# Blocked causal attention: GpSimd zeroes the masked half of the diagonal blocks after the exponential, in place of TensorE's mask products of the second pass

## The reference, cut to what matters

```python
x = x + 0.5 * L0_ffn(layernorm(x))
x = x + L0_attn(layernorm(x), w_qkv, w_out)   # the stage of this change
x = x + 0.5 * L0_ffn(layernorm(x))            # ... and eight more stages
# inside L0_attn, for one batch of 256 tokens and one head:
# scores = q @ k.T * HD ** -0.5; a query sees the keys up to its own place
# att = softmax(scores) @ v ; all heads' att @ w_out
```

## Time and profile before

| what | value |
|---|---|
| median of 3 runs | 3186.45 us (3180.18 to 3190.23) |
| span of the profiled execution | 3040.8 us |
| PE busy | 2525.0 us (83%) |
| DVE busy | 2108.5 us (69%) |
| ACT busy | 1803.5 us (59%) |
| POOL busy | 1186.1 us (39%) |
| pass B's mask products, PE busy (L2004) | 47.2 us, 512 products of 178 ns |

### The profile page before, as it was taken

How to read it: one execution, slowest core, us unless ns; L and a number is a source line. 1 busy time by engine, 2 the same in 40 slices (tenths; PEclk the granted TensorE clock), 3 DMA queues, 4 the chain that set the end, 5 groups by cost and what they waited for, 6 DMA issues and landing times.

```text
span 3040.8 us, 67855 instructions
## 1 busy us (share of the span) xinstructions
PE 2525.0 (83%) x25429; PEld 1994.5 (66%) x25429; DVE 2108.5 (69%) x7749; ACT 1803.5 (59%) x3508; POOL 1186.1 (39%) x1634
## 2 busy tenths in 40 slices
PE   7889989759599777569489999999999986693886
PEld 4466665447377555346378999999999874462655
DVE  6667765863378833854488888888888887445877
ACT  5344445434255333446279999999999974462553
POOL 4200002576532657566662222222222235656412
PEclk9799998879799788779799999999999997796997
DMA  9900000014210133325100000000000001351001
GB/s 237 283 19 3 3 3 1 13 54 141 68 48 3 40 106 114 97 83 177 55 27 13 2 13 10 4 14 1 13 14 1 2 1 34 102 168 41 27 3 29
DMA packets 148390, 157.20 MB, mean 52 GB/s; under 512 B 15585, under 2 KB 123746, under 8 KB 148066
## 3 DMA queue, kind: packets, MB, share of 16 engines
q1 hardware_dynamic: 119618, 78.14, 9.6%
q0 software_dynamic: 28448, 74.71, 7.7%
HBM read 77.79 MB, written 75.01 MB: 50 GB/s over the span
## 4 chain that ended last, share of the span: by engine, by line
PE 39%; DVE 11%; POOL 5%; issue 3%; DMA 1%; ACT 1%; POOLq 0%; DVEq 0%; ACTq 0%
PE banks L3246 7%; PE banks L3261 7%; PE banks L3191 3%; POOL bins L2984 3%; PE banks L3227 2%; PE banks L3200 2%; PE banks L3208 2%; PE banks L3226 2%; PE banks L3184 2%; PE banks L3022 1%; PE banks L3023 1%; PE banks L3033 1%; PE banks L3024 1%; PE banks L3035 1%; POOL results L1441 1%
## 5 line engine op out<-in xcount | busy, mean ns | idle before, releaser
L3343 POOL TENSOR_SCALAR shared_floats<-shared_floats 128x2 f32<-128x2 f32 x256 | 57.3, 224 | 658.1 <-DVE shared_floats L3334 657.9
L3261 PE MATMUL banks<-layer,shared_floats 128*128 128x128 f32 x2048 | 291.2, 275 | 0.0
L3261 PEld LDWEIGHTS banks<-layer,shared_floats 128*128 128x128 f32 x2048 | 258.8, 192 | 0.0
L3246 PE MATMUL banks<-shared_floats,layer 128*128 128x256 f32 x1024 | 245.8, 383 | 0.0
L3582 ACT ACTIVATE shared_floats<-banks,layer 128x256 f32<-128x256 f32 x512 | 210.2, 470 | 52.1 <-PE banks L3246 52.1
L3246 PEld LDWEIGHTS banks<-shared_floats,layer 128*128 128x128 f32 x1024 | 187.6, 193 | 20.8
L3345 POOL TENSOR_TENSOR shared_floats<-shared_floats,neg_half 128x2 f32<-128x2 f32 x256 | 183.2, 715 | 21.3
L1361 POOL DMA_INDIRECT results<-shared_floats,e_token_rows x160 | 155.0, 969 | 88.3 <-issue 48.2
L3355 DVE TENSOR_SCALAR shared_floats<-banks,shared_floats 128x128 f32<-128x128 f32 x512 | 185.8, 404 | 4.0 <-POOL shared_floats L3345 4.0
L244 PE MATMUL banks<-ident,xn 128*128 128x128 f32 x320 | 62.3, 327 | 141.5 <-issue 81.6
L2133 DVE TENSOR_REDUCE shared_floats<-banks 128x2 f32<-128x512 f32 (+3 forms) x256 | 110.7, 484 | 94.2 <-PE banks L1997 93.0
(11 more groups left out here) (398 smaller groups left out, 7968.0 us busy)
## 6 DMA issues: line engine op xcount, KB each, us to landing
bins<-zero SPq DMA_DIRECT2D x1, 18176.0 KB, 69.5
bins<-layer SPq DMA_DIRECT2D x16, 650.0 KB, 12.2
shared_floats<-bins SPq DMA_DIRECT2D x32, 325.0 KB, 3.4
expert_weights<-in_dram_experts SPq DMA_DIRECT2D x32, 312.0 KB, 3.0
results<-results SPq DMA_DIRECT2D x32, 256.0 KB, 3.2
layer<-in_dram_layers SPq DMA_DIRECT2D x8, 902.0 KB, 4.5
results<-zero SPq DMA_DIRECT2D x1, 4096.0 KB, 16.1
bins<-xn,f_bin_row POOLq DMA_INDIRECT x256, 2.3
```

Source lines behind the costliest of these rows:

```text
L3246: m = T.matmul(k.bank[5 + half][:, part], w["w1"][:, tile(n)], h1[:, :], start=True, stop=True)
L3261: m = T.matmul(to, hidden[:, n * S + t * P:n * S + (t + 1) * P], w["w2"][:, tile(n)], start=False, stop=(n == NF - 1), skip_group_check=True)
```

## The change

The mask products of pass B (L2004) are gone; the product that subtracts the maxima now ends the group (`stop=True`), and it raises `at_scored_b`. The exponential is therefore taken of unmasked scores. The eight exponential buffers become slices of one tensor, `at_exps`, so that two neighbouring ones can be reached in one instruction. GpSimd gets `mask_exps`: for each pair of exponentials it waits for `at_exps`, then issues for each block of the round four `affine_select` instructions, one for each 32 partitions, on 2 x 32 columns (the diagonal block in both buffers), which put zero where the key is ahead of the query. The last one raises a semaphore (`constants_made`, from 2 on). `weigh` waits for that semaphore and no longer for `at_exps`. The norm's roots on GpSimd are moved into the same list of jobs, at the job "stats", behind a wait for all masking issued so far, and each is followed by a wait for its own end.

```diff
--- before.py
+++ after.py
@@ -1945,6 +1945,15 @@
 
     return [k.sb(f"at_{name}{c % 2}", [P, width]) for name, width in
             (("q", CH), ("k", CH), ("q_heads", 4 * CH), ("k_heads", 4 * CH), ("v_heads", 4 * CH))]
+
+
+def att_exps(k, unit):
+    return k.sb("at_exps", [P, 8 * CH])[:, unit % 8 * CH:(unit % 8 + 1) * CH]
+
+
+def exps_masked(k):
+
+    return k.sem("constants_made"), 2
 
 
 def softmax_tensor(k, s, a):
@@ -1998,11 +2007,8 @@
                                    mask(k, "ahead_a", r)[:, 0:ahead], start=False, stop=True, skip_group_check=True)
             if i < len(blocks_b):
                 for r in rows_b:
-                    T.matmul(k.bank[6 + r % 2][:, at_b:at_b + wide_b], mask(k, "minus", r),
-                             shifts[rows32(r), begin_b:end_b], start=False, stop=False, skip_group_check=True)
-                for r in rows_b:
-                    m_b = T.matmul(k.bank[6 + r % 2][:, at_b:at_b + BK], mask(k, "same", r), mask(k, "ahead_b", r),
-                                   start=False, stop=True, skip_group_check=True)
+                    m_b = T.matmul(k.bank[6 + r % 2][:, at_b:at_b + wide_b], mask(k, "minus", r),
+                                   shifts[rows32(r), begin_b:end_b], start=False, stop=True, skip_group_check=True)
                 at_b += wide_b
         if first is not None:
             m_a.then_inc(k.sem("at_scored_a"), 1)
@@ -2020,10 +2026,11 @@
             if n:
                 T.wait_ge(k.sem("at_att"), a.g0 + n)
         if begin == 0:
-            T.wait_ge(k.sem("at_exps"), a.u0 + n * a.units + 4 * rd + 4)
+            masked, made = exps_masked(k)
+            T.wait_ge(masked, made + n * a.slots + 2 * rd + 2)
         for b, first, last in blocks[begin:end]:
             blk, width = n % 2 * BLOCKS + b, last - first
-            exps = [k.sb(f"at_exps{(n * a.units + 4 * rd + r) % 8}", [P, CH])[:, at:at + width] for r in range(4)]
+            exps = [att_exps(k, n * a.units + 4 * rd + r)[:, at:at + width] for r in range(4)]
             begins, ends = first == 0, b == BLOCKS - 1
             for r in range(4):
                 T.matmul(to[rows32(r), first:last], v_heads[:, blk * P + 32 * r:blk * P + 32 * r + 32], exps[r],
@@ -2235,7 +2242,7 @@
         if 2 * g >= 8:
             A.wait_ge(k.sem("at_weighed"), a.r0 + (2 * g - 8) // 4 + 1)
         for r in rows:
-            A.activation(k.sb(f"at_exps{(n * a.units + 4 * rd + r) % 8}", [P, CH])[:, 0:width],
+            A.activation(att_exps(k, n * a.units + 4 * rd + r)[:, 0:width],
                          k.bank[6 + r % 2][:, 0:width], ACT.Exp, scale=SCALE).then_inc(k.sem("at_exps"), 1)
 
     def copy_shifts(n):
@@ -2268,10 +2275,42 @@
 
 def softmax_gpsimd(k, s, a):
 
-    for c in range(s.early, NC):
-        ln_rstd(k, s, c)
-    for j in range(NC):
-        early_root(k, s, j)
+    G, (masked, made) = k.nc.gpsimd, exps_masked(k)
+
+    def mask_exps(n, p):
+
+        n, rd, rows, g = a.pair(n, p, True)
+        unit = (n * a.units + 4 * rd + rows[0]) % 8
+        both = k.sb("at_exps", [P, 8 * CH])[:, unit * CH:(unit + 2) * CH].rearrange("p (r n) -> p r n", n=CH)
+        G.wait_ge(k.sem("at_exps"), a.u0 + 2 * g + 2)
+        at = 0
+        for _, first, last in a.rounds_b[rd]:
+            for j in range(4):
+                block = both[rows32(j), :, at:at + BK]
+                m = G.affine_select(out=block, in_=block, compare_op=ALU.is_ge, fill=0.0, base=0,
+                                    pattern=[[0, 2], [1, BK]], channel_multiplier=-1)
+            at += last - first
+        m.then_inc(masked, 1)
+
+    if not s.early:
+        ln_rstd(k, s, 0)
+        G.wait_ge(k.sem("ln_rstd"), s.ln(0) + 1)
+    for n in range(B + a.lag):
+        c, odd = n // 2, n % 2
+        for job, i, behind in a.order:
+            if job == "score" and a.pair(n, i, True) is not None:
+                mask_exps(n, i)
+            if job == "stats":
+                done = sum(a.pair(m, p, True) is not None for m in range(n + 1) for p in range(a.slots) if (m, p) < (n, 2))
+                if done:
+                    G.wait_ge(masked, made + done)
+                if max(s.early, 1) <= c + 1 < NC and not odd:
+                    ln_rstd(k, s, c + 1)
+                    G.wait_ge(k.sem("ln_rstd"), s.ln(c + 1) + 1)
+                if n >= 2 * NC - 2:
+                    early_root(k, s, n - (2 * NC - 2))
+                    if s.next and n - (2 * NC - 2) < s.next.early:
+                        G.wait_ge(k.sem("ln_rstd"), s.next.ln(n - (2 * NC - 2)) + 1)
 
 
 CAUSAL_A = [[(b, 0, 256) for b in (6, 7)], [(b, 0, 192) for b in (4, 5)],
```

## The result

The changed kernel took 3252.11 us (median of 4 runs, 3247.22 to 3252.18) against 3183.31 us of the kernel before (median of 4, 3173.89 to 3190.23): ratio 1.0228, 95% interval 1.0206 to 1.0249. It is 69 us or 2.3% slower. The forecast was 3198 us, with a range up to 3233.

A forecast was written before the change was run, and what follows sets the result against it. PE was taken to set the pace, with DVE close behind. Contention 8 x 1.7 = 13.6, plus 1.5 at the stage's end, less 3.5 gained, gave +11.6 us: 3186.45 to 3198 us, range 3180 to 3233.

The forecast's parts named there:

- the selects run one by one: Rival for the selects on POOL: start-to-start spacing 0.19 to 0.24 us, total 3218 to 3233 us, chance 0.23.
- The bound of the pace: Selects on POOL: start-to-start spacing x lies between 0.04 and 0.24 us, from memsets and one 128 x 128 select.
- x = 0.13: Selects on POOL: forecast start-to-start spacing in us, near the middle of the bounds, as four neighbours may overlap.
- quadrants running side by side: Rival for the selects on POOL: full overlap of the four gives x = 0.08 and 3187 us, chance 0.33.
- 0.16 + 11x + 0.28: Masks ahead of `weigh`: us from the exponentials until a burst of 12 selects is ready, x being their start-to-start spacing.
- taken at nothing: Wait of `weigh` in round 0: no cost, with only 8 selects against a slack of about two scores.
- the late `weigh` of round 1 lies in the same stretch of the loop and hides in it: Wait of `weigh` in round 1: late by 0.1 and 0.2 us, adding nothing beyond the 1.7 us charged for contention.
- The contention: DVE's `parts` beside a burst of selects: 1.1 us overlap per batch, 1.7 us per two batches after cover, 13.6 in all.
- behind DVE's addition of 0.69 us as well: Term of the one-by-one rival: round 1's burst delayed by DVE's addition in one batch of two, 8 x 0.69 us.
- The end of the stage: Where the batches run out: fewer jobs between exponential and `weigh` cost 1.5 us, between 0 and 4.
- The gain: Removal of 512 mask products from PE: 3.5 us saved, with ends 0 and 4.8, from 0.03 us per pair.
- The roots at "stats": Norm's roots on POOL, with the next masks behind them: no cost unless x is over 0.19.

The follow-up runs named there:

- e6_whole: Changed kernel with one always-true select per block over all 128 partitions instead of four over 32, pass B unmasked: 3035.03 us, ratio 0.9981 to the kernel before.
- e9_by_quadrant: Changed kernel with the same 1024 selects issued quadrant by quadrant instead of block by block: 3210.43 us against 3177.49 of the kernel before, ratio 1.0095.
- e10_scratch_roots: Kernel before plus 1024 selects on a scratch tile, awaited only by GpSimd, roots issued ahead of round 2's second burst: 3181.87 us against 3177.49, ratio 1.0013.
- e5_after_again: The changed kernel, unedited, run again: 3114.32 us against 3041.59 of the kernel before, ratio 1.0246.
- e1_before_again: The kernel before, unedited, traced again on a quicker chip: span 3036.5 us, 3037.96 us in the run beside it.
- e2_no_masking: Changed kernel without the GpSimd selects, pass B unmasked, weigh waiting for the exponentials: 3030.72 us against 3039.37 of the kernel before, ratio 0.9967.

## Why the prediction was wrong

The direction and the mechanism (selects one by one, `weigh` waits for them) were in it, as the rival "the selects run one by one", with a chance of 0.23 and 3218 to 3233. The forecast itself, +11.6 us, was built on another mechanism: it was contention between the selects and DVE's `parts` (13.6 us of it), with the wait of `weigh` put at nothing. What the runs show is the reverse, a wait of 6.4 us in two batches and little contention. The measured 69 us lie above the whole range, the rival included. By steps:

1. **The bound of the pace.** "These bound the pace x ... 0.04 to 0.24 us" failed. The upper end was the spacing behind one select of 128 x 128, with twice our elements in each partition and four times the partitions, and so it looked safe. Measured: 0.28. From start to start it is 0.19, as estimated for one alone, as long as the next one works on the same partitions; with a change of quadrant the next starts 0.05 us after the last has ended. The row of the bound had a successor that works on all partitions as it does, and could not show this.

2. **Where I took the middle.** x = 0.13 rested on quadrants running side by side in part. No overlap of quadrants shows in any trace. The rule of the Trainium skill that spoke for it ("GPSIMD Engine Reference", section Instruction dispatch: a core begins the next instruction as soon as its own share of the last is done) is not borne out in its effect here: e6_whole and e9_by_quadrant show that neighbours on different partitions follow each other later than those on the same.

3. **The wait, and that it would hide.** The formula 0.16 + 11x + 0.28 was right: with 0.28 it gives 3.5 us, and 3.44 to 3.45 were measured. Round 1 is late by 1.7 us, round 2 by 0.9 and more, and even round 0, "taken at nothing", by 0.2: its 8 selects are ready 2.41 us behind the exponentials, against a slack of 2.13 to 2.25 us before. What failed is "the late `weigh` of round 1 lies in the same stretch of the loop and hides in it". It doesn't hide: PE's idle time in two batches goes from 3.4 to 9.1 us, 6.4 more by the new wait and 0.7 less by the old ones. With 0.8 us of products gone that makes 4.9, and 43.93 - 39.07 is 4.9. The rival left the wait of round 1 out of its sum too: with 0.28 for x its terms give some +53 us (an estimate: 8 x 3.9 of contention, 16 x 1.0 for round 2, 8 x 0.69, 4, less 3.5), still too low, and with contention as the largest of them.

4. **The contention.** 1.1 us for each batch at x = 0.13 (up to 2.2 at 0.24) was the largest term, and it failed. The wait for DVE's maxima was to grow from 3.3 us to about 5 and shrank to 2.4. DVE's `parts` in the changed kernel starts at 318.21 and its last four products are over at 320.59:

```profile
318.21 0.17 DVE L2158 CAST at_high<-shared_floats 128x32 bf16<-128x32 f32 x1
...
320.05 0.54 DVE L2161 TENSOR_TENSOR at_parts<-shared_floats,same_head 128x32 bf16<-128x32 f32 x4
```

It takes 2.38 us instead of 2.19, and 2.48 in every second batch, while POOL issued select after select. The longest of its products takes 0.27 us in the changed kernel against 0.19 before. A small operation that meets a select is held up by some tens of ns, at most 0.08 us. The earlier trace rows showed the hold-up behind a POOL operation with two inputs over all partitions, and I carried it over to selects with one input over a quarter of them; which of the two differences matters was not tried. All contention of DVE with the selects together is some 4 us or less (e10_scratch_roots).

   The other way round there is a hold-up that the forecast left out and the rival named ("behind DVE's addition of 0.69 us as well"). DVE's addition over 128 x 512, both inputs in SBUF, makes the select that starts inside it take up to 0.64 us instead of 0.23, 12 times in the stage. Here the first select of a burst starts 0.23 us behind the addition's start, and the burst of 12 takes 3.65 us instead of 3.32:

```profile
310.83 0.69 DVE L2129 TENSOR_TENSOR shared_floats<-shared_floats 128x512 f32<-128x512 f32 x1
...
311.06 3.65 POOL L2290 TENSOR_SCALAR_AFFINE_SELECT shared_floats<-shared_floats 32x64 f32<-32x64 f32 x12 [1.16 <-ACT shared_floats L2245]
```

   Where such a burst is one that `weigh` waits for, in round 2 of every second batch, `weigh` starts 3.85 us behind the exponentials and not 3.45.

5. **The clock, which was not in the sum.** In the changed kernel PE is granted the lower level now and then from about 177 us on; the kernel before has 1.00 in all windows of its steady part. Two batches with such stretches take 45.59 and 47.15 us against 43.93 without: 1.7 and 3.2 us. From `parts` of the second batch to `parts` of the last, 14 batches, it is 321.3 us in e5_after_again (175.6 to 497.0, mean clock 0.94) against 269.7 in e1_before_again (176.4 to 446.2, mean clock 0.99), 51.6 more. Seven times 4.9 is 34, which leaves some 18 us for the clock; at a mean clock of 0.94 the work of PE loses 6% of 321 us, 19 us, which is about as much. The four runs of e5_after_again point the same way: the one of this trace, with a mean clock of 0.907 over the program, took 3105.83 us, the three with 0.896 and 0.897 took 3112.58 to 3119.09.

   What PE did before the falls was to stand in the waits for GpSimd that the kernel before doesn't have: in the trace of the changed kernel each of the eight falls between 200 and 440 us comes 1.4 to 2.8 us after the start of such a wait of 1.35 to 1.73 us. But the same waits stand between 315.67 and 359.60 us, where the clock stays at 1.00, so they are not enough by themselves. With the shorter bursts of e9_by_quadrant, PE's longest idle time there is 1.35 us, and the clock kept 1.00. That the waits are the cause is the likeliest reading, not a shown one, since no run kept the waits and filled them with work for PE.

6. **The end of the stage.** 1.5 us was the estimate, 4 the upper end. From `parts` of the last batch to the last product of `weigh` it takes 35.3 us in e5_after_again (mean clock 0.65) against 21.6 in e1_before_again (0.92), 13.8 more. But the trace of before takes 31.8 us for it at a clock of 0.54, and the changed kernel's first trace 36.4 at 0.56. So at like clocks it is some 5 us, and the rest is a clock that differs between two executions of the kernel before as well, by 10 us.

7. **The gain.** 3.5 us, 4.8 at most; measured 8.7 (e2_no_masking), of which the steady part shows 6.2. 0.03 us for a pair of products was the gap from its start to the next product's, but a score with round 1 is 0.15 us shorter (1.55 to 1.40), 0.05 for each of its three blocks, and one with round 0 is 0.13 shorter (1.43 to 1.30). Scores with round 2 stay at 1.26, as forecast. The weight load between the two products went as well, and I hadn't counted it; that it makes the difference between 0.03 and 0.05 was not tried.

8. **The roots at "stats".** "Nothing, unless x is over 0.19" was right as a condition, and x is over it. In the changed kernel DVE waits for them for 8.3 us between 160 and 440 us (e5_after_again), against 0.5 before.

The sum as measured, from two traces of quicker chips, e5_after_again against e1_before_again: the spans differ by 67.9 us (3104.4 and 3036.5). Of these 34 come from longer pairs of batches (waits for POOL less gains), some 18 from the clock, and 14 from the end of the stage, most of these from the clock too. That makes 66, while the start of the stage is 0.8 us shorter; the stage itself is 64.3 us longer (420.0 against 355.7). The 3.6 us beyond it are within what such runs scatter.

## What to carry to other kernels

Ask of a moved operation first how late its result may come: `weigh` had 1.7 us of slack; with 6 selects ahead of it the kernel was as fast as before, with 12 it was 73 us slower. Then charge that lateness in full unless a row shows what it hides behind. Count the instructions, not the elements: a mask as one multiplication over all partitions did the same work in 3 instructions, and was 0.24% faster than the kernel before where the 12 selects were 2.3% to 2.5% slower. And a bound for the pace of an operation holds only if the row that it is taken from also has the same kind of neighbour.

## What the runs showed of the hardware

- GpSimd follows a select with one on the same partitions 0.19 us after its start, before its end; with one on other partitions 0.28 us after its start, 0.05 us after its end as the profile has it (64 elements for each partition, 32 or 128 partitions). Order alone took the loss from 69 us to 33 us, on chips of the slower kind.
- A select over 32 partitions takes up to 0.64 us instead of 0.23 when it starts inside a 0.69 us addition of DVE with both inputs in SBUF. The small products of `parts` take at most 0.27 us instead of 0.19 beside such selects.
- PE's granted clock fell to the lower level, 1.2 GHz, for stretches in the middle of the stage in the kernel whose PE stood in waits of up to 1.7 us for GpSimd before, though not behind every such wait; a pair of batches then took 1.7 and 3.2 us more than 43.93.
- The same program takes 3040 us on one chip and 3180 us on another, with the difference in the routed stages.
